# GpSimd adds pairs of key banks and TensorE's key sums stream half the columns in three quarters of each image

## The reference

```python
xn = group_norm(x, gn1_w, gn1_b)
q, k, v = split(conv1x1(xn, w_qkv))      # 4 heads of 32, 4096 tokens
q = elu(q) + 1.0
k = elu(k) + 1.0
k_sum = k.sum(axis=tokens)               # what the change touches
kv = einsum('bhnd,bhne->bhde', k, v)
out = (q @ kv) / (q . k_sum + 1e-6)      # per token and head
out = group_norm(conv1x1(out, w_out), gn2_w, gn2_b) + x
```

## Time and profile before

| | us |
|---|---|
| median of 3 runs | 667.65 (665.71, 667.65, 667.80) |
| span of the profiled execution | 664.7 |
| TensorE busy | 632.9 (95%) |
| VectorE busy | 568.4 (86%) |
| ScalarE busy | 428.5 (64%) |
| GpSimd busy | 128.2 (19%) |
| mean granted TensorE clock | 0.988 |

### The profile page before, as it was taken

The page is one execution under the profiler, slowest core; times in us unless marked ns, Lnnn a source line. Parts: engine busy times, 40 slices in busy tenths (PEclk is TensorE's granted clock), DMA queues, the critical chain, the costliest instruction groups (busy, mean ns, idle before and its releaser), DMA issues.

```text
span 664.7 us, 27754 instructions
## 1 busy us (share of the span) xinstructions
PE 632.9 (95%) x10562; PEld 539.5 (81%) x10562; DVE 568.4 (86%) x1953; ACT 428.5 (64%) x1062; POOL 128.2 (19%) x112
## 2 busy tenths in 40 slices
PE   7799999999999999999999999998989999999991
PEld 5799999999999899999999999965646656655650
DVE  5689989999899888989999999989868778878784
ACT  3456666677777766666665666657666867867744
POOL 0022200000000000000000000000153666666654
PEclk9999999999999999999999999999999999999996
DMA  9999990233333100000000000000326368468546
GB/s 173 207 207 186 165 178 0 52 81 80 81 79 82 41 1 0 0 0 0 0 2 0 0 0 0 0 1 2 73 70 148 78 131 179 101 125 182 115 83 127
DMA packets 79314, 50.38 MB, mean 76 GB/s; under 512 B 44256, under 2 KB 72352, under 8 KB 79264
## 3 DMA queue, kind: packets, MB, share of 16 engines
q1 hardware_dynamic: 75936, 48.91, 36.6%
q10 hardware_dynamic: 3328, 0.82, 0.6%
HBM read 32.34 MB, written 9.24 MB: 63 GB/s over the span
## 4 chain that ended last, share of the span: by engine, by line
PE 49%; DVE 32%; issue 10%; ACT 3%; DMA 3%; DVEq 1%; POOL 1%; ACTq 0%; SPq 0%; POOLq 0%
PE bank L549 33%; DVE scan_rows L840 7%; DVE parts L813 7%; DVE parts L840 7%; PE bank L680 3%; DVE fin L927 2%; PE bank L630 2%; DVE rows_h L1004 2%; PE bank L616 2%; DVE stats L1045 2%; DVE kp L994 1%; PE bank L669 1%; PE bank L634 1%; PE bank L604 1%; DMA rows_h<-bounce 1%
## 5 line engine op out<-in xcount | busy, mean ns | idle before, releaser
L549 PE MATMUL bank<-parts 128*128 128x124 f16 (+2 forms) x7560 | 421.4, 219 | 7.5 <-issue 4.2
L549 PEld LDWEIGHTS bank<-parts 128*128 128x128 f16 x7560 | 415.4, 98 | 14.0 <-issue 5.7
L1222 ACT ACTIVATE parts<-parts 128x128 f16<-128x128 f16 x506 | 156.6, 310 | 150.0 <-DVE parts L840 125.1
L813 DVE TENSOR_TENSOR parts<-scan_rows,parts 128x128 f16<-128x128 f32 x506 | 148.9, 294 | 14.2
L840 DVE SCALAR_TENSOR_TENSOR parts<-bank,cols_w 128x128 f16<-128x128 f32 x378 | 109.5, 290 | 22.3 <-PE bank L549 7.1
L840 DVE SCALAR_TENSOR_TENSOR scan_rows<-bank,cols_w 128x128 f32<-128x128 f32 x378 | 105.9, 280 | 0.0
L442 POOL TENSOR_TENSOR scale<-dev,half 128x2 f32<-128x2 f32 (+1 forms) x2 | 2.1, 1036 | 401.5 <-DVE dev L952 401.5
L453 POOL TENSOR_TENSOR rows_h<-rows_h 128x512 f32<-128x512 f32 x52 | 67.9, 1339 | 47.3 <-DMA rows_h<-bounce 47.3
L994 DVE SCALAR_TENSOR_TENSOR kp<-ex,bank 128x512 f32<-128x512 f32 x64 | 40.8, 679 | 21.3 <-ACT ex L1355 20.9
L1233 ACT ACTIVATE cols_w<-scan_rows 128x256 f32 x126 | 52.5, 417 | 5.7 <-issue 0.2
L1361 ACT ACTIVATE ex<-bank,minus_one 128x512 f32<-128x512 f32 x64 | 40.6, 689 | 14.6 <-PE bank L616 14.6
(11 more groups left out here) (146 smaller groups left out, 591.6 us busy)
## 6 DMA issues: line engine op xcount, KB each, us to landing
rows_h<-bounce SPq DMA_DIRECT2D x52, 256.0 KB, 4.8
cols_w<-x SPq DMA_DIRECT2D x6, 896.0 KB, 12.0
ex<-scan_rows SPq DMA_DIRECT2D x84, 64.0 KB, 2.0
out<-fin SPq DMA_DIRECT2D x10, 512.0 KB, 7.3
cols_w<-x SPq DMA_DIRECT2D x12, 384.0 KB, 8.6
cols_w<-x SPq DMA_DIRECT2D x12, 256.0 KB, 6.3
cols_w<-x SPq DMA_DIRECT2D x6, 512.0 KB, 10.5
kp<-scan_rows SPq DMA_DIRECT2D x40, 64.0 KB, 1.9
```

The source lines that it names most:

```text
L549: last = nc.tensor.matmul(conv_rows[g][u % SLOTS][:, :, to], w[:, k, d, :], rows_16[:, u % SLOTS, g * GB:(g + 1) * GB, of], start=part_n = ...
L813: nc.vector.tensor_tensor(low[:, slot, gb, :], state[:, slot, gb, :] if row is None else row[:, gb, :], high[:, slot, gb, :], ALU.subtract ...
L1222: act.activation(high_down[:, slot, gb, :], high[:, slot, gb, :], ACT.Copy, scale=1.0 / LOW_SCALE).then_inc(down_ready[g], 1)
```

## The change

Three edits:

1. A tile `kp_pair` of 128x512 in a free part of `scan_rows`, and a semaphore `paired`. GpSimd's `pair_of_keys(b, i)` adds the two key buffers of quarter i into it, for i = 0, 1, 2, after both keys are ready and after the gather before has read the last pair. TensorE's gather of those quarters then waits for `paired` after its key-times-token products and sums 128 columns for each column group instead of 256, into `acc_ps[:, P:2P]`. Quarter 3 is as before.
2. GpSimd's order in one iteration is: the second half's four products of the previous iteration, pair 0, the scale and shift of the previous iteration, pair 1, the residual sum, pair 2, the first half's four products. The last scale and shift follows after the loop.
3. The scale of the first normalisation for images 2 to 7 moves from before the loop into iteration 1, after pair 0.

```diff
--- before.py
+++ after.py
@@ -137,6 +137,8 @@
 
         fin_tail = recip_b.rearrange("p u n -> p (u n)").rearrange("p (c j w) -> p c j w", c=2, j=J)
         back_to_heads = scan_rows[:, 0:SUBS * P].rearrange("p (s n) -> p s n", s=SUBS)
+
+        kp_pair = scan_rows[:, SUBS * P:SUBS * P + CHUNK]
         back_ps = (key_ps[0], key_ps[1], query_ps[0], query_ps[1], acc_ps, out_ps, key_ps[0], tok_ps)
         back_before_ps = (key_ps[0], key_ps[1], tok_ps, query_ps[0])
         last_den_ps = (small_ps, acc_ps)
@@ -217,6 +219,7 @@
         first_high, first_low = sem("first_high"), sem("first_low")
         yn_ready, tok_done, tok_ready = sem("yn_ready"), sem("tok_done"), sem("tok_ready")
         key_done, key_exp, kp_ready, acc_used = sem("key_done"), sem("key_exp"), sem("kp_ready"), sem("acc_used")
+        paired = sem("paired")
         query_done, query_exp, qp_ready = sem("query_done"), sem("query_exp"), sem("qp_ready")
         acc_read, small_done, small_read = sem("acc_read"), sem("small_done"), sem("small_read")
         recip_ready, normed, norm2 = sem("recip_ready"), sem("normed"), sem("norm2")
@@ -445,7 +448,6 @@
                                         ALU.mult).then_inc(ready, 1)
 
             scale_of(FIRST, var_ready, scale_ready)
-            scale_of(REST, rest_var_ready, rest_scale_ready)
 
             def normalise_units(b, par, m):
                 at_least(pool, recip_sent[m], 64 * b)
@@ -477,20 +479,35 @@
                     cols[:, :, bass.ds(b - 2, 1), :].rearrange("p w o j -> p w (o j)"), ALU.add)\
                     .then_inc(fin_ready, 1)
 
+            def pair_of_keys(b, i):
+
+                at_least(pool, kp_ready, KBANKS * b + 2 * i + 2)
+                at_least(pool, acc_used, 4 * b + i)
+                nc.gpsimd.tensor_tensor(kp_pair, kp[:, (2 * i) % 4, :], kp[:, (2 * i + 1) % 4, :], ALU.add)\
+                    .then_inc(paired, 1)
+
+            def scale_when_known(b, par):
+                at_least(pool, small_read, small_step(b, 5))
+                scale_and_shift(b, par)
+
             def iteration(b, par, cur, prev, pp):
 
+                if pp:
+                    normalise_units(b - 1, 1 - par, 1)
+                pair_of_keys(b, 0)
+                if prev and not pp:
+                    scale_of(REST, rest_var_ready, rest_scale_ready)
+                if has_finished(b):
+                    scale_when_known(b - 1, 1 - par)
+                pair_of_keys(b, 1)
                 if has_finished(b):
                     finish(b - 1, 1 - par)
+                pair_of_keys(b, 2)
                 if prev:
                     normalise_units(b, par, 0)
-                if prev and has_next(b, cur):
-                    normalise_units(b, par, 1)
-                if pp:
-
-                    at_least(pool, small_read, small_step(b, 5))
-                    scale_and_shift(b, par)
 
             batches(pool, iteration)
+            scale_when_known(B - 1, 1)
             for h, rows in enumerate(HALVES):
                 pool.wait_ge(affine_done, B - 2 + h)
                 pool.wait_ge(stored, (B - 1) * 32 - 63)
@@ -630,10 +647,17 @@
                         nc.tensor.matmul(acc_ps[d * C:(d + 1) * C, 0:P], tok[:, i % 2, n * P + d * C:n * P + (d + 1) * C],
                                          kp[:, (2 * i + d) % 4, n * P:(n + 1) * P],
                                          start=i == 0 and n == 0, stop=i == 3 and n == 3, skip_group_check=True)
+                if i < 3:
+                    at_least(pe, paired, 3 * b + i + 1)
                 for n in range(4):
-                    last = nc.tensor.matmul(acc_ps[DH * n:DH * (n + 1), P:3 * P], ones[:, :],
-                                            kp[:, (2 * i + n // 2) % 4, (n % 2) * 2 * P:(n % 2 + 1) * 2 * P],
-                                            start=False, stop=i == 3, skip_group_check=True)
+                    here = slice(DH * n, DH * (n + 1))
+                    if i < 3:
+                        last = nc.tensor.matmul(acc_ps[here, P:2 * P], ones[:, :], kp_pair[:, n * P:(n + 1) * P],
+                                                start=False, stop=False, skip_group_check=True)
+                    else:
+                        last = nc.tensor.matmul(acc_ps[here, P:3 * P], ones[:, :],
+                                                kp[:, (2 * i + n // 2) % 4, (n % 2) * 2 * P:(n % 2 + 1) * 2 * P],
+                                                start=False, stop=True, skip_group_check=True)
                 last.then_inc(acc_used, 1)
 
             def sums(to):
```

## The result

The changed kernel takes 691.75 us (690.12 to 692.92, 4 runs) against 667.72 us of the kernel before beside it: ratio 1.0357, 95% interval 1.0337 to 1.0376, so 24 us slower. The forecast was slower, 677.0, with a range up to 683. The sign was right and so was the place, the seam between GpSimd's two halves and VectorE's subtractions; the measured loss is 2.6 times the forecast 9.3 us. The profiled execution took 691.09 us with a span of 689.2.

What follows compares the result with a forecast made beforehand. The prediction saw two tied 24.5 us loops, TensorE's order and one through the affine, VectorE and GpSimd's products. Four turns (8.0), approach (1.1) and tail (0.2) gave + 9.3 us, time 677.0, range 668 to 683.

Steps and rivals of the forecast that it cites:

- The chain leaves TensorE between the affine and the group mean: Attention turns: cheaper key sums save about 0.29 us a gather, but lie off the chain there, so none was counted.
- Pair 0 stands in the loop: Between GpSimd's second-half products and the scale, pair 0 delays the next affine by 1.3 us a turn.
- Residual sum, pair 2 and first products run back to back to affine + 16.7: GpSimd's order after pair 1: first products run from + 11.7 to + 16.7, where before they started at + 9.2.
- The 0.4 us of idle GpSimd: Gap between first products' end, + 16.7, and second half's landing, + 17.1; deducted from the collision bound, 1.7 to 1.3 a turn.
- VectorE beside GpSimd: VectorE's two subtractions fall on the seam between GpSimd's product halves: 0.7 us a turn taken, bounds 0 to 1.3.
- Rival C: VectorE and GpSimd exclude one another in full, normalisation included: + 14.7 us, time 682; chance 0.15.
- Approach + 1.1: Up to the first affine: + 1.3 for pair 0, + 0.4 for the normalisation's collision, - 0.6 from image 0.
- the normalisation collision: Whole-image normalisation against pair 0 and scale: + 0.4 in the approach; 0 taken in turns, 1.2 kept for the range.
- the 0.6 gain in image 0: VectorE waits 0.61 us behind TensorE's queries in image 0; cheaper gathers were to save 0.6 once.
- Tail + 0.2: After the last affine: first products end at + 16.7, the output product started at + 16.5; + 0.2, bound + 1.
- The 3 us around the span: Some 3 us between profiled span, 664.7, and measured median, 667.65; forecast span 674.0 thus gave time 677.0.
- The signs: Expected in the profile: affines 26 to 27.3 us apart, GpSimd idle under 2 a turn, ScalarE's longest wait the affine's for the scale.

Runs made afterwards that it cites:

- e4: Changed kernel's pair sums and half key sums, but in the previous kernel's GpSimd order, pairs in its idle stretches: 669.77 us, ratio 1.0044.
- e7: e4 without pair sums in image 0: 667.79 us, ratio 0.9993 against the kernel before.
- e2: Changed kernel, with GpSimd starting the second half's four products only after VectorE's two low-half subtractions of that image: 684.88 us, ratio 1.0250.
- e8: e2 with pair 0 moved behind the scale and shift instead of ahead of it: 678.46 us, ratio 1.0149.
- e3: Changed kernel without the pair sums and half key sums, keeping GpSimd's new order: 668.06 us, ratio 1.0004.
- e10: Changed kernel with GpSimd waiting for its own fourth product, between the two halves' products: 682.49 us, ratio 1.0203.
- e13: Changed kernel with GpSimd waiting for its own last first-half product, placed after the sixth of the eight products: 684.66 us, ratio 1.0264.
- e6: Changed kernel without pair sums in image 0, new order kept: 686.01 us, ratio 1.0249, runs from 681.4 to 690.8.
- e5: Micro-benchmark, not the kernel: two VectorE subtractions beside nine GpSimd products, arrival moved in 18 steps; first took 2.27 us down to 1.21, second 2.28.
- e9: Micro-benchmark nearer the kernel: subtractions behind the kernel's own VectorE instructions, beside later products, behind a long sum, in a loop; none was shut out.
- e11: e7 with GpSimd's scale and shift between the halves' products and ScalarE's affine between its two copies of quarter 0: 666.76 us, ratio 0.9979.

## Why the prediction was right in sign and wrong in size

- **The chain leaves TensorE between the affine and the group mean, so the cheaper sums gain nothing in a turn.** Right: e4 and e7 have them and turns of 24.5. The sums' own size was off, 0.17 us a gather instead of 0.29; in the turns nothing hung on it.
- **Pair 0 stands in the loop, 1.3 us a turn.** Right in size: 1.2 (e2 against e8), and the affine waits for the scale by up to 2.16 us. In the two long turns of the changed kernel it was not in the loop: pair 0 itself waited 6.4 us for VectorE's keys, and the affine waited for nothing.
- **Residual sum, pair 2 and first products run back to back to affine + 16.7.** Right in order; the first products began at 537.44, affine + 11.7, as worked out. The 0.4 us of idle GpSimd that I counted behind them was there in image 4 (0.38) and not in images 3 and 5, where the second half's data had landed by then; I took it for a saving, and it was the gap in which VectorE runs. That the new order costs by itself was not claimed, and e3 confirms it.
- **VectorE beside GpSimd, "I take 0.7", with bounds 0 to 1.3 a turn.** This is the step that failed, in its size and in its upper bound. It added up the durations of the instructions that meet, as if each could cost the other no more than itself. Where I had 4 x 0.7 = 2.8 us for the four turns, the runs leave 19.4 - 4 x 1.2 = 14.6. In the changed kernel the subtraction stayed out until the run of products ended, in two of four images (6.86 and 6.87 us instead of 1.2): 8.8 us of turns, clock included. The rest is over the bound of 1.3 a turn too, 1.9 in e2 and e8 and 1.45 in e10, though under the 2.5 that it makes with the 1.2 kept for the scale and the normalisation; these do meet, where I had taken 0. The rows of before could not show the shut-out: there never were eight products in one run. Rival C, at 682, had the exclusion in full, but with one instruction as the most that it could cost.
- **TensorE stays at full clock.** I never asked, and so put it at nothing. By the estimate from the chain it is some 4.2 us of the 8.8. The waits of 4.5 us before 548.5 and 606.9 were both followed by the lower level, in e13 one of two waits of 2.1 us was; the rows of before held no such wait in the turns.
- **Approach + 1.1.** It was 4.0 (81.4 against 77.4 us from first scale to first affine). Pair 0 gave its 1.3; the normalisation collision, taken at half, came nearly in full (the scale's first instruction took 1.60 us at 523.04 instead of 0.58); the 0.6 gain in image 0 did not come, and some 1.7 us more were lost. Pair 0 of image 0 met a subtraction which I had not looked for, since it belongs to the first image alone; e6, without pairs there, has 1.8 us less from scale to affine, but how much of it is the clock stays open.
- **Tail + 0.2.** It was 0.1.
- **The 3 us around the span.** They are 1.9 in the changed kernel's profiled execution and 2.0 or so in all others; the forecast time doesn't hang on it, as it is the median before plus 9.3.
- **The signs.** Affines 26 to 27.3 us apart were seen in two of four turns. That GpSimd would be idle under 2 us a turn, and that ScalarE's longest wait would be the affine's, failed in the long turns (GpSimd 6.4 us for the keys, ScalarE 4.6 for TensorE).

By turns: 19.4 us measured = 8.8 shut-out and clock (e10) + 4 x 1.2 pair 0 (e2 against e8, taken to cost the same in e10) + 5.8 for the rest of the seam; forecast 8.0 = 4 x 1.3 + 4 x 0.7.

What stays open: why the first break decides. In e5 and e9 alone, 29 trials beside runs of nine products, VectorE got in behind the product that was running each time. In the kernel it did so too as soon as the run had one break. Something in the kernel's run of eight, which my trials lack, keeps it out before that. That the break cures it is shown by e10 and e13; the reason is not.

## What to carry to other kernels

Before work is put on GpSimd beside VectorE, look where VectorE has instructions with two SBUF inputs, and what waits for them; idle time of GpSimd is no cover if the new work closes the gap in which VectorE used to run. Don't bound such a meeting by the durations of the two instructions: an unbroken run of GpSimd instructions can cost all that is left of it, as it did here and not in the small trials, so look at the trace. A wait of GpSimd for itself in the middle of the run, or for VectorE's instruction, was worth more here than it cost. And an engine that is busy 99% of a stretch need not be the one whose instructions end the chain: ask where the chain leaves it before giving it less to do.

## What the runs showed of the hardware that I had not expected

- One VectorE subtraction (1.2 us alone) took 6.86 and 6.87 us beside a run of 128x512 GpSimd products, and 2.0 or 4.4 with a break in the run. The Trainium skill's "whole instruction" in "SBUF — State Buffer" holds in all the micro-benchmarks and not in this case; the measurement decides for this kernel.
- A GpSimd instruction on one column waits too: the scale's first took 1.49 us beside a subtraction (e11) and 1.60 beside the normalisation, instead of 0.58.
- After 4.5 us without work TensorE ran at the lower level, once for about 3 us (0.57 granted from 548 to 552 us) and once for about 6 (0.51 and 0.64 from 606 to 614). After 2.1 us without work it did so once (e13, 0.83 and 0.74 from 544 to 552) and once not (1.00 from 600 to 608).
